# A transformer block on one core: setup moved behind the first projections, two operations moved to other engines, a scan in the entmax, and an order of work planned with later arrivals

## What is computed

```python
x = x + _L0_attn_ref(_layernorm(x), w_qkv, w_out)          # 16 heads of 16, causal softmax
x = x + _L0_ffn_ref(_layernorm(x), ...)                    # gates by entmax15 over 16 logits, R = 128, O = 1024, gelu
x = x + _L1_attn_ref(_layernorm(x), Wq_down, ..., Wc)      # low-rank q, k, v; rotary on half of each head
x = x + _L1_ffn_ref(_layernorm(x), Ws1, Ws2, W1, W2, Wr)   # shared expert, plus routed experts whose weight reaches 1
```

```python
zs = -jnp.sort(-z, axis=-1)
mean = jnp.cumsum(zs, axis=-1) / k
meansq = jnp.cumsum(zs * zs, axis=-1) / k
```

## Time and profile before

| | us |
|---|---|
| median of 3 runs | 3171.22 |
| lowest and highest | 3166.03, 3175.09 |
| the profiled execution, its own time | 3174.84 |
| its span, first to last instruction | 3173.1 |
| PE busy (share of the span) | 2888.2 (91%) |
| DVE busy | 2165.5 (68%) |
| ACT busy | 1905.3 (60%) |
| POOL busy | 1138.1 (36%) |
| mean granted clock of TensorE | 0.950 of full |

### The profile page before, as it was taken

The page is one execution under the profiler, slowest core; times in us unless marked ns, Lnnn a source line. Parts: engine busy times, 40 slices in busy tenths (PEclk is TensorE's granted clock), DMA queues, the critical chain, the costliest instruction groups (busy, mean ns, idle before and its releaser), DMA issues.

```text
span 3173.1 us, 55225 instructions
## 1 busy us (share of the span) xinstructions
PE 2888.2 (91%) x17687; PEld 1366.4 (43%) x17687; DVE 2165.5 (68%) x5957; ACT 1905.3 (60%) x3740; POOL 1138.1 (36%) x2476
## 2 busy tenths in 40 slices
PE   5787999999899998999989998999989999899996
PEld 3433443445344453445534454344534445344432
DVE  4573687765878558775577766776677865878582
ACT  3455655766466664767547674675746766466654
POOL 2314441435324342244513355132541435324421
PEclk9888999999899998999989999999989999899998
DMA  5602442323424253333514245132442324423230
GB/s 153 157 19 64 94 101 50 82 74 99 103 60 106 58 132 73 67 82 93 132 38 89 59 118 126 36 84 56 116 119 54 87 71 116 96 59 83 67 86 22
DMA packets 241196, 268.25 MB, mean 85 GB/s; under 512 B 19568, under 2 KB 208912, under 8 KB 240912
## 3 DMA queue, kind: packets, MB, share of 16 engines
q1 hardware_dynamic: 240912, 264.66, 35.5%
HBM read 162.35 MB, written 100.66 MB: 83 GB/s over the span
## 4 chain that ended last, share of the span: by engine, by line
PE 63%; DVE 18%; ACT 10%; issue 3%; DMA 3%; SPq 2%; POOL 1%; ACTq 0%; POOLq 0%; DVEq 0%
PE ps L1134 14%; PE ps L1116 13%; PE ps L1092 10%; PE ps L1072 6%; DVE mx L1691 6%; PE ps L1064 5%; ACT probs L1428 5%; DVE ps L1688 4%; PE ps L1210 4%; PE ps L1205 3%; PE ps L1197 2%; PE ps L1052 2%; DMA stk_k<-k 1%; ACT xn L1377 1%; PE ps L1097 1%
## 5 line engine op out<-in xcount | busy, mean ns | idle before, releaser
L1428 ACT ACTIVATE probs<-ps 128x512 f32<-128x512 f32 (+1 forms) x2432 | 1228.9, 595 | 429.0 <-PE ps L1116 421.6
L1691 DVE TENSOR_REDUCE mx<-ps 128x1 f32<-128x512 f32 (+2 forms) x1408 | 893.8, 683 | 238.8 <-PE ps L1092 132.6
L1092 PE MATMUL ps<-stk_k,stk_q 112*128 112x512 bf16 (+3 forms) x3072 | 809.9, 339 | 94.2 <-DVE mx L1691 31.2
L1595 POOL TENSOR_SCALAR_AFFINE_SELECT probs<-probs 128x128 f32<-128x128 f32 (+2 forms) x1408 | 479.9, 349 | 866.0 <-ACT probs L1428 836.5
L1116 PE MATMUL ps<-stk_q,stk_k 115*128 115x512 bf16 (+3 forms) x3072 | 758.3, 332 | 27.5 <-DMA stk_q<-mT 21.0
L1688 DVE CUSTOM_DVE_ANT_0 ps<-ps,mask_b 128x512 f32<-128x512 f32 (+1 forms) x1024 | 613.3, 649 | 137.7 <-PE ps L1092 133.2
L1134 PE MATMUL ps<-probs,vaug 128*17 128x512 f32 (+3 forms) x6144 | 586.9, 494 | 11.2 <-ACT probs L1428 6.7
L1092 PEld LDWEIGHTS ps<-stk_k,stk_q 112*128 112x128 bf16 x3072 | 276.4, 98 | 510.1 <-issue 363.5
L1116 PEld LDWEIGHTS ps<-stk_q,stk_k 115*128 115x128 bf16 x3072 | 269.0, 98 | 451.3 <-issue 206.2
L1064 PE MATMUL ps<-turned,wqkv 128*128 128x512 f32 x512 | 269.6, 615 | 9.9 <-ACT turned L1364 5.8
L1134 PEld LDWEIGHTS ps<-probs,vaug 128*17 128x17 f32 x6144 | 138.2, 97 | 313.3 <-issue 188.4
(11 more groups left out here) (155 smaller groups left out, 3128.3 us busy)
## 6 DMA issues: line engine op xcount, KB each, us to landing
k<-parts SPq DMA_DIRECT2D x128, 384.0 KB, 3.5
stk_q<-q SPq DMA_DIRECT2D x256, 192.0 KB, 4.1
stk_k<-k SPq DMA_DIRECT2D x128, 384.0 KB, 6.7
q<-parts SPq DMA_DIRECT2D x64, 384.0 KB, 3.0
stk_k<-k SPq DMA_DIRECT2D x128, 192.0 KB, 4.2
x<-in_L_attn_x SPq DMA_DIRECT2D x16, 512.0 KB, 4.9
k<-parts SPq DMA_DIRECT2D x64, 128.0 KB, 3.5
stk_q<-q SPq DMA_DIRECT2D x128, 64.0 KB, 6.2
```

The costliest lines, as they stand in the source:

```text
L1092: ins = pe.matmul(out[:, width * a:width * (a + 1)], q, stk_k[0:ROWS_S, slot, h + a, BANK * p:BANK * p + width], start=a == 0, stop=a == n ...
L1428: act.activation(probs[:, step % PBUF, h:h + k, cols], src, ACT.Exp, scale=SCALE)\
L1595: pool.affine_select(out=diag, in_=diag, compare_op=ALU.is_ge, fill=0.0, base=0, pattern=[[0, k]] * (k > 1) + [[1, P]], channel_multiplier ...
L1691: dve.tensor_reduce(most, tile.rearrange("q (k w) -> q k w", k=k), AX.X, ALU.max)\
```

## The change

Seven things change together.

1. **The start.** `setup` becomes the last step of the chain that also holds the projections of chunk 0 of sequence 0; the projections of chunk 1 are another chain and come first. The scores wait in the plan until `setup` is done.
2. **Costs of the plan.** `later()` adds 1.5 to the assumed arrival of the first `xt` of a normalisation, 0.7 to `yt` and `at`, and `ROWS_LATER` adds 1.5 to the landing of the row of maxima. The costs of `rot`, `add` and `mt` follow the moves below.
3. **The sine product** goes from VectorE to GpSimd, where it stands in front of the add, in the step `add`.
4. **The copy into `mT`** goes from VectorE to ScalarE.
5. **The running sums** become one `tensor_tensor_scan` over 128 elements, in which a factor tile `going` (0 at the first of every 16, else 1) restarts the sum.
6. **Fill.** Where the plan has PE idle over 0.25 before the first `xt`, `yt` or `at`, or before the first `st` of a unit, it notes one filler for each 0.25. There, PE claims the item's PSUM tile before the item's wait, and multiplies a constant bf16 mask by an identity into the tile, which the item then overwrites. There are 178 of them at 30 places.
7. **The router's weights** stand in the upper half of `projw` instead of a tile of their own; the product has the same size.

```diff
+SETUP_TIME, SETUP_LOADED = 20.0, 20.0
...
-    "rot": (0.0, ("DVE", 1.5), ("POOL", 1.0)), "add": (0.0, ("POOL", 1.2)), "p0": (0.0, ("ACT", 0.63)),
+    "rot": (0.0, ("DVE", 0.75), ("POOL", 1.25)), "add": (0.0, ("POOL", 2.6)), "p0": (0.0, ("ACT", 0.63)),
...
+LATER = {"xt": 1.5, "yt": 0.7, "at": 0.7}
+ROWS_LATER = 1.5
...
-    out = [([], [], loaded(0, 0) + loaded(0, 1) + projection(0, 0, 0)), ([(0, 0, 0)], [], projection(0, 0, 1))]
+    out = [([], projection(0, 0, 1), loaded(0, 0) + loaded(0, 1) + projection(0, 0, 0) + [([("setup",)], "")]),
+           ([(0, 0, 0)], [], loaded(1, 0) + projection(1, 0, 0))]
...
+        time += later(step)
...
-        end = self.on("DVE", self.pe + HOP, 0.4)
+        end = self.on("ACT", self.pe + HOP, 0.6)
...
-        self.rows[u] = self.transfer(end, 1.4, 0.1)
+        self.rows[u] = self.transfer(end, 1.4, 0.1) + ROWS_LATER
...
-        if u not in self.rows:
+        if u not in self.rows or ("setup",) not in self.at:
...
+            item = plan.chains[args[0]][0][0][0]
+            if item[0] in ("xt", "yt", "at") and gap > FILL_TIME:
+                FILL[item] = int(gap / FILL_TIME)
...
+            def keep_going(key, pt):
+                if FILL.get(key, 0) and key == next(iter(FILL)):
+                    pe.wait_ge(pool_chain, 8)
+                for _ in range(FILL.get(key, 0)):
+                    pe.matmul(pt, ident_b[:], mask_b[:], start=True, stop=True)
...
             def transposed_x(n, b, c, kd):
+                pt, done = claim(("xt", n, b, c, kd))
+                keep_going(("xt", n, b, c, kd), pt)
                 pe.wait_ge(xn_ready, 2 * (LN["rstd", n, b, c] + 1))
-                pt, done = claim(("xt", n, b, c, kd))
...
+                out, done = claim(("st", u, j, h))
                 if j == 0 and h == 0:
+                    keep_going(("st", u, j, h), out)
                     pe.wait_ge(m_loaded, 16 * (MT["mt", u] + 1))
-                out, done = claim(("st", u, j, h))
...
+            def max_rows(u):
+                pt = arrived(act, ("mt", u))
+                if MT["mt", u]:
+                    act.wait_ge(m_loaded, 16 * MT["mt", u])
+                act.activation(mT[:], pt[0:NP * HG, 0:BANK // 2].bitcast(BF16), ACT.Copy).then_inc(read_out(("mt", u)), 1)
...
             def rotate(*key):
                 o, r, w = PROJ["qk", *key], ROPE["rot", *key], key[4]
+                pool.wait_ge(swap_ready, r + 1)
+                pool.tensor_tensor(qs[w], qs[w], sin[:, BANK * key[2]:BANK * (key[2] + 1)], ALU.mult).then_inc(sin_ready, 1)
                 pool.wait_ge(cos_ready, r + 1)
...
-                dve.wait_ge(swap_ready, r + 1)
-                dve.tensor_tensor(qs[w], qs[w], sin[:, BANK * key[2]:BANK * (key[2] + 1)], ALU.mult).then_inc(sin_ready, 1)
...
+                    flat = [v.rearrange("p t k -> p (t k)") for v in (going[:], cum[:, 0], cum[:, 2])]
+                    link(dve.tensor_tensor_scan(flat[2], flat[0], flat[1], 0.0, ALU.mult, ALU.add))
                 elif part == 4:
-                    a = cum[:, 2]
-                    for r, s in enumerate((4, 8)):
-                        z = cum[:, 1 + r % 2]
-                        dve.tensor_copy(z[:, :, 0:s], a[:, :, 0:s])
-                        link(dve.tensor_tensor(z[:, :, s:E0], a[:, :, s:E0], a[:, :, 0:E0 - s], ALU.add))
-                        a = z
```

More of the change, by code:

```diff
@@ L162, in loaded @@
     return before + [([("load", b, c)], ""), ([("stat", b, c)], "")]
+SETUP_TIME, SETUP_LOADED = 20.0, 20.0
 TIMES = {
     "most": (0.0, ("DVE", 0.19)), "mx": (0.0, ("POOL", 1.15)),
-    "load": (0.0, ("SP", 6.0)), "stat": (0.0, ("DVE", 2.2)), "rstd": (0.0, ("POOL", 1.35)), "norm": (0.0, ("ACT", 0.8)),
+    "setup": (SETUP_TIME,), "load": (0.0, ("SP", 6.0)), "stat": (0.0, ("DVE", 2.2)), "rstd": (0.0, ("POOL", 1.35)), "norm": (0.0, ("ACT", 0.8)),
     "xt": (0.44, ("ACT", 0.6)), "yt": (0.44, ("ACT", 0.6)), "qk_": (0.86,), "qk": (0.86, ("ACT", 0.9)),
-    "rot": (0.0, ("DVE", 1.5), ("POOL", 1.0)), "add": (0.0, ("POOL", 1.2)), "p0": (0.0, ("ACT", 0.63)),
+    "rot": (0.0, ("DVE", 0.75), ("POOL", 1.25)), "add": (0.0, ("POOL", 2.6)), "p0": (0.0, ("ACT", 0.63)),
     "rest": (0.0, ("POOL", 1.16)), "p1": (0.0, ("ACT", 0.63)), "p2": (0.0, ("POOL", 1.16)),
@@ L220, in windows @@
         else:
-            out.append(([(0, 0, 1)], attended(0, 0, 0) + first_ffn(0, 0), ahead + first))
+            out.append(([(0, 0, 1)], attended(0, 0, 0) + first_ffn(0, 0), first))
             out.append(([(0, 1, 0), (1, 0, 0)], attended(0, 0, 1) + first_ffn(0, 1), second))
@@ L271, in chain_time @@
         time = self.ready[n]
+        if step[0] and step[0][0][0] == "setup":
+            return max(time, SETUP_LOADED)
+        time += later(step)
         for item in step[0]:
@@ L310, in give @@
                     self.open[n] = b
+            if item[0] == "setup":
+                self.busy["ACT"] = self.busy["DVE"] = self.pe
+                self.free = [min(end, self.pe) for end in self.free]
             for engine, length in rest:
@@ L471, in normalise, with later @@
         self.put(("nm", u), end)
+def later(step):
+    item = step[0][0] if step[0] else ("",)
+    return 0.0 if item[0] in ("xt", "yt") and item[-1] else LATER.get(item[0], 0.0)
 def takes_time(step):
@@ L507, in late @@
         return line - (starts[u] - LEAD - score_work(u) * n / len(score_items(u)) * SPREAD)
-    position = 0
+    position, gap = 0, 0.0
     while main or todo or any(plan.chains) or plan.held or plan.outputs:
@@ L537, in program_order @@
                     moved = True
-        if setup:
-            plan.put(("setup",), plan.pe)
-            plan.pe += 18.0
-            plan.free = [min(time, plan.pe) for time in plan.free]
-            for engine in ("ACT", "DVE"):
-                plan.busy[engine] = plan.pe
-            setup = False
         plan.load_stack()
@@ L589, in program_order @@
             plan.pe = max(plan.pe, time) + (0.001 if what == "wait" else 0.0)
-            IDLE.append((now, plan.pe - now, what if isinstance(what, str) else what.__name__, args))
+            gap += plan.pe - now
         if what == "wait":
@@ L598, in program_order @@
                 begins[u] = plan.pe
+            if j == 0 and h == 0 and gap > FILL_TIME:
+                FILL["st", u, j, h] = int(gap / FILL_TIME)
             plan.scores_t(u, j, h)
@@ L606, in program_order @@
             what()
+        if what != "wait":
+            gap = 0.0
     order = plan.order
@@ L617 @@
 EARLY = True
+FILL_TIME = 0.25
+FILL = {}
 PLACE = {}
-IDLE, FINISH = [], []
+FINISH = []
 ORDER = program_order()
@@ L775, in transformer_kernel @@
         gate = sb("gate", [P, B, TT, NE])
+        going = sb("going", [P, 2 * TPC, E0])
         gmax = sb("gmax", [P, NC * B])
@@ L1145, in transposed_y @@
             def transposed_y(b, l, c, kd):
+                pt, done = claim(("yt", b, l, c, kd))
+                keep_going(("yt", b, l, c, kd), pt)
                 in_sbuf(pe, ("nm", LAST_UNIT[b, l, c]))
-                pt, done = claim(("yt", b, l, c, kd))
                 for i in range(TPC):
@@ L1179, in transposed_a @@
             def transposed_a(b, c):
+                pt, done = claim(("at", b, c))
+                keep_going(("at", b, c), pt)
                 pe.wait_ge(a_ready, ENT["epow", b, c] + 1)
-                pt, done = claim(("at", b, c))
                 for i in range(TPC):
@@ L1494, in _ @@
                     exponentials(*key)
+                elif kind == "mt":
+                    max_rows(*key)
                 elif kind == "o":
@@ L1873, in fold @@
                 copy(wout2T[:], D)
-            for w in (projw, wr):
-                dve.memset(w[:], 0.0)
+            dve.memset(projw[:], 0.0)
             dve.memset(up, 0.0).then_inc(up_zeroed, 1)
+            dve.memset(going[:, :, 1:E0], 1.0)
+            dve.memset(going[:, :, 0:1], 0.0)
             dve.memset(vaug[:], 1.0)
@@ L1898, in _ @@
                     greater(*key)
-                elif kind == "mt":
-                    max_rows(*key)
                 elif kind == "nm":
```

23 lines of the change are left out of this document (4 added, 19 removed).

## The result

The changed kernel was run four times, at 3033.6, 3035.3, 3038.4 and once, in a slow run that no ratio uses, at 13351.9 with a granted clock of 0.19. The recorded median of all four, 3036.9 us, is the figure from here on, against 3172.3 for the kernel before, timed beside it; the median of the three is 3035.3, so differences from 3036.9 carry some 2 us. The ratio is 0.9572, with a 95% interval of 0.9552 to 0.9593: 135 us less.

The account below looks back on a forecast made before the run. VectorE at 97% bounds six 24 us half-clock stretches, PE others, the entmax wait a third kind. Terms -75 - 24 - 3 + 12 + 3 + 2 + 2 = -83 gave 3092 us, 3088 for the median; range 3040 to 3145.

Parts of the forecast that it names:

- R4: Rival: slower, sine products in GpSimd's in-order queue delay the masks, so pv and st wait; 3242 us, chance 0.09.
- R2: Rival: whole loss goes, clock never falls in the six stretches and at is covered wholly; 3049 us, chance 0.17.
- (e): Copy into mT on ScalarE: VectorE loses 52.3 us, ScalarE gains 128 copies; forecast +3 us (0 to +13).
- (f): Sine product on GpSimd: VectorE loses 51.7 us, GpSimd gains 81, masks queue behind it; forecast +2 us (0 to +10).
- (a): Six half-clock stretches before the first st: 27 of 44 score tiles move beside the pass ahead; -75 us (-93 to -40).
- R1: Rival: the bound moves along, PE may wait where the scores now stand, half of (a) stays; 3125 us, chance 0.20.
- (b): Entmax before at, six places: scan shortens the chain by 1.3 us, steps stand later; -24 us (-45 to -10).
- (c): Start: both projections before the fold, first st near 93 to 98 instead of 106; -3 us (-12 to +8).
- (g): Fillers: 178 at about 0.22 us, free in real waits, delaying PE where it comes late; +2 us (0 to +10).
- (d): The end: chain of the last sequence's chunk 0 moves to a place with no cover; +12 us (+5 to +20).

Follow-up runs that it names:

- new_order_old_engines: Changed kernel, order kept item by item, but sine product, copy into mT and running sums back on VectorE in their old form: 3109.5 us, ratio 0.981.

## Why the prediction was off, point by point

**What held.** The places were right. The 24 us stretches at half clock vanished, the rows of maxima are waited for no more, `at` waits under 2 us, and the scan is at 424 ns in 11 places of 16, near the 0.5 I took (its mean is 721). At the start the first `xt` is at 27.1 (forecast 27), the second at 45.4 and the fold at 60.0 (63), the first score at 77.3 (80) and the first `st` at 97.9 (93 to 98). R4 had no part in it: `pv` waits 6.6 us more for GpSimd in all, and just as much (10.2) in `new_order_old_engines`, where GpSimd has no sine product; and the product there is worth 22 us. The rule of the Trainium skill ("SBUF — State Buffer", "Who interferes with whom") stood against that move, 3130 by my reading; the trace does not bear out its cost. In the same lines as the earlier trace rows, the operation that took 874 ns at the worst now never does, and in `new_order_old_engines` it does not either (3.6 us for all 16), so the order alone did that:

```profile
L1773 DVE TENSOR_TENSOR zt<-zc x16: 224/225/230, 182.1 to 2772.9; 128x64 f32<-128x64 f32 x16
```

In R2 the prediction says that the six stretches agree with the Trainium skill on waits that bring the throttle back ("TensorE: Matmul & The Clock Gate", "HAM oscillation — how this bites in real kernels"). The trace bears this out in part: the page describes one long wait ahead of each cold burst, and here PE had only short ones. In the 38.4 us from 791 to where the clock falls, at 829.4, it waited 5.2 us in all, and longest here:

```profile
829.14 0.38 PE L1092 MATMUL ps<-stk_k,stk_q 112*128 112x512 bf16 x1 [1.58 <-DVE mx L1691]
```

**Where it failed: the terms (e) and (f), and that the parts add.** The runs split the change in two. For all but the moved copy and product I had forecast -75 - 24 - 3 + 12 + 2 = -88, in which the scan has some 8 (1.3 at six places); the order with the new start and the fillers, but without the scan, measured -61. For the copy and the product I had forecast +5; with the scan they measured -17 in the old order and -73 in the new. So the order gave 27 us less than its terms and the moves 78 more, which is how 83 became 135. The separate gains, 61 and 17, add up to 78, close to my sum, and that is luck: one group was forecast too high and the other with the wrong sign. What was missing from the sum is the 57 us that come only with both.

I priced the copy by its own length on ScalarE (+3) and the product by the queue on GpSimd (+2). What VectorE has less to do I had put at nothing, but for a bit in (a). The runs show 0.33 to 0.40 us for each us of VectorE, in either order, so 52 + 52 us are some 35 to 40; and for the copy about 23 more that time alone does not explain, most likely by when it starts, because on VectorE it stood behind reductions (not shown by a run of its own). In the new order (e) is -48 and (f) -22. They are not to be added to (a): half of the regular period's gain appears only once the moves are in (368.5 with the order alone, 376.4 with the moves alone, 358.3 with both, from 379.8).

**(a), the scores moved ahead.** I had 15.5 us of loss in each stretch, 9.5 of them by 27/44 of the tiles, and took 12.5, between that and all. That went by how many scores the new order put in the stretch and not by what else: the chain's products stand among the 17 tiles that are left. The half clock there goes almost whole with the order alone, as R2 had it. The waits do not: with the order alone they fall from 23.7 to 18.9 us in a period, as R1 had it, and a period gains 11.3 us, less than the 16.5 of (a) and (b) together. With the moves as well it gains 21.5, near the (93 + 45) / 6 = 23 of R2.

**(c), the start,** forecast -3, is +3 to +5: inside its ends, wrong in sign. **(g), the fillers,** forecast to cost 2, save 4 to 6, of which I had counted 2 to 3 in (d). **(d), the end,** forecast +12, was not measured apart. The moved chain does stand bare (without fillers PE waits 10.45 us for its `xn`, at 2891.5), but the last 484 us became 18 shorter, where (a), (b) and (d) together had 4 or 5. **The scan** is worth 11 us in the new order; (b) as a whole was not measured apart, because its order part is the planner's.

**What the arrivals do.** LATER and ROWS_LATER are worth 44 and 67 us, each with the other on. Without either the planner's order is irregular. With ROWS_LATER at 0 the six stretches hold 45, 24, 52, 14, 24 and 52 score tiles, and the first five periods take 378, 353, 394, 359 and 352 us, a mean of 367; with both numbers it is 17 six times and 358. With LATER off they hold 15, 16, 19, 15, 16 and 19, and the periods take 372, 367, 355, 371 and 367. So the number of tiles in a stretch does not order the periods: 24 tiles go with the shortest, 352 and 353, and 15 with 372. Nor is it regularity alone, since the kernel before has 44 each time and is the slowest. The regular orders with few tiles have the best means, but what makes them so was not tested by itself.

**Open.** What exactly makes copy and order worth more together. In the old order the traces put the copy's loss at the half clock that ends later and at the wait for `xn`; the new order has no such stretch, but no run separates that from the rest. The scan alone was not run in the old order. Two causes that I proposed, a standing queue and a higher price of VectorE's time, were tested and fell. The later row of maxima with the `stk_k` loads behind it, which the waits show in the new order, is also left, and no run changed it by itself.

## What to carry to other kernels

When an order of work changes, look at what now stands beside the work that used to be bare, not only at how much of it is left. Here the clock's share of the loss went with the order alone, and more of the waits only when VectorE also had less to do. Work on an engine that looks off the path is not free: here each us of it cost a third to two fifths of one. An operation's price has three parts: its time on the engine, when it can start there, and what of the same queue comes later. A copy of 52 us in all was worth 48 in one order, where time alone would make it about 20. Small moves and a new order should be priced together, since here one of them was worth 7 us of loss under one order and 48 of gain under the other.

## What the runs showed of the hardware

The same `tensor_tensor_scan` over 128x128 took 423 to 426 ns in 11 places of the changed kernel and 1315 to 1395 in 5. In this run all 16 are at the shorter time:

```profile
L1798 DVE TENSOR_TENSOR_SCAN cum<-going,cum x16: 424/424/425, 194.5 to 2810.4; 128x128 f32<-128x128 f32 x16
```

It is the changed kernel with two added copies for each unit on VectorE; the copies themselves took 206 to 1332 ns there, with a median of 226. The order of work is the same, so the second duration wanders from one operation to another as the timing shifts. For the scans of the changed kernel it makes 4.8 us of VectorE in all (11.5 busy, against 6.8). A copy of 12x512 bf16 out of PSUM took 579 ns on ScalarE and 408 on VectorE, and in the new order it was still the better for it.
